# Interleaved attention and FFN block: the order of the work lists of TensorE, ScalarE and VectorE

## The reference

```python
xn = _layernorm(x)
# attention, on _rmsnorm(xn, norm_w)
q = x @ Wq; k, v = split(x @ Wkv)               # 16 heads of 64
q = _head_rmsnorm(q, q_gamma); k = _head_rmsnorm(k, k_gamma)
sim = jnp.tanh(q @ k.T / 50.0) * 50.0 * 64 ** -0.5
out = (softmax(sim) @ v) @ Wo
# FFN, m1 and m2 are products of token rows of the batch
h = gelu(x @ W1.T + scale * (x @ m1.T) + b1)
ffn = h @ W2.T + scale * (h @ m2.T) + b2
return x + out + ffn
```

## Time and profile before

| | |
|---|---|
| median of three executions | 1172.26 us |
| the profiled execution | 1171.93 us, span 1170.0 us |
| granted clock of TensorE | 0.996 of full speed |
| PE busy | 1053.4 us (90%) |
| ACT busy | 1033.3 us (88%) |
| DVE busy | 932.8 us (80%) |
| POOL busy | 853.8 us (73%) |

### The profile page before, as it was taken

One profiled execution on the slowest core, in us unless ns is written; L12 is line 12 of the kernel. 1 busy time (PEld: TensorE's weight loads), 2 busy tenths in 40 slices (PEclk: granted clock), 3 DMA queues, 4 the chain that ended last, 5 costly groups with the idle time before them and its releaser, 6 DMA issues.

```text
span 1170.0 us, 33883 instructions
## 1 busy us (share of the span) xinstructions
PE 1053.4 (90%) x12873; PEld 833.1 (71%) x12873; DVE 932.8 (80%) x2185; ACT 1033.3 (88%) x1543; POOL 853.8 (73%) x784
## 2 busy tenths in 40 slices
PE   3779999999999999999999999999999999999987
PEld 2457777777777777777777777777777777777766
DVE  5887878887878878878878878878888878888862
ACT  2689999999999999999999999999999999999886
POOL 6577777778778777778777778777778777778654
PEclk9899999999999999999999999999999999999999
DMA  4244443334433333434334433334333334343341
GB/s 142 42 78 67 77 74 77 68 74 74 77 77 74 70 70 78 74 75 77 72 66 79 76 72 79 66 74 79 74 72 78 71 69 83 70 75 70 71 81 33
DMA packets 310743, 86.45 MB, mean 74 GB/s; under 512 B 282036, under 2 KB 309816, under 8 KB 310584
## 3 DMA queue, kind: packets, MB, share of 16 engines
q1 hardware_dynamic: 310584, 84.30, 37.7%
HBM read 12.13 MB, written 4.19 MB: 14 GB/s over the span
## 4 chain that ended last, share of the span: by engine, by line
ACT 34%; PE 26%; DVE 26%; issue 12%; DMA 0%; POOL 0%; ACTq 0%
ACT clamped L569 12%; PE ps_scores L492 9%; DVE qk L764 7%; ACT probs L576 7%; PE ps_aux L467 5%; DVE halves L728 5%; ACT oT L608 4%; ACT L613 4%; DVE o_sb L741 3%; PE ps_y L542 3%; DVE v_lo L769 3%; DVE norm L679 3%; ACT hid L613 3%; PE ps_y L540 3%; PE ps_aux L426 2%
## 5 line engine op out<-in xcount | busy, mean ns | idle before, releaser
L931 POOL TENSOR_TENSOR probs_lo<-probs 128x1024 f16<-128x1024 f32 x256 | 484.7, 1893 | 270.3 <-ACT probs L576 270.3
L569 ACT ACTIVATE clamped<-ps_scores 128x1024 f32<-128x1024 f32 x256 | 265.9, 1039 | 67.2 <-PE ps_scores L492 66.9
L576 ACT ACTIVATE probs<-clamped 128x1024 f32<-128x1024 f32 x256 | 275.4, 1076 | 1.0 <-PE ps_o L522 0.4
L728 DVE TENSOR_TENSOR halves<-ps_n,halves 128x512 f16<-128x512 f32 x256 | 175.1, 684 | 99.3 <-ACT halves L584 99.2
L520 PEld LDWEIGHTS ps_o<-v_hi,probs 128*128 128x128 bf16 x2048 | 184.7, 98 | 90.0 <-issue 87.5
L520 PE MATMUL ps_o<-v_hi,probs 128*128 128x65 bf16 x2048 | 214.0, 195 | 33.2 <-DVE ps_n L720 23.1
L492 PE MATMUL ps_scores<-heads_T 64*128 64x256 f16 x3072 | 212.8, 271 | 6.9 <-ACT clamped L569 4.7
L521 PE MATMUL ps_o<-v_lo,probs 128*128 128x64 bf16 x2048 | 212.2, 193 | 0.0
L522 PE MATMUL ps_o<-v_hi,probs_lo 128*128 128x65 bf16 x2048 | 211.9, 194 | 0.0
L426 PE MATMUL ps_aux<-w_hi,xhT_hi 128*128 128x512 f32 x384 | 174.4, 454 | 40.0 <-DVE v_lo L769 25.6
L521 PEld LDWEIGHTS ps_o<-v_lo,probs 128*128 128x128 bf16 x2048 | 187.5, 99 | 0.0
(11 more groups left out here) (80 smaller groups left out, 1919.4 us busy)
## 6 DMA issues: line engine op xcount, KB each, us to landing
heads_T<-halves SPq DMA_TRANSPOSE x512, 2.5
x_in<-in_L_attn_tokens_dram SPq DMA_DIRECT2D x32, 128.0 KB, 2.3
x_res<-in_L_attn_tokens_dram SPq DMA_DIRECT2D x32, 128.0 KB, 2.3
out_dram<-y_sb SPq DMA_DIRECT2D x32, 128.0 KB, 2.0
sel_raw<-xn SPq DMA_DIRECT2D x192, 4.0 KB
qk<-in_L_attn_Wkv_dram SPq DMA_DIRECT2D x2, 512.0 KB, 5.2
qk<-in_L_attn_Wq_dram SPq DMA_DIRECT2D x1, 512.0 KB, 4.0
qk<-in_L_ffn_W_dram SPq DMA_DIRECT2D x2, 256.0 KB
```

The costliest lines, as they stand in the source:

```text
L569: nc.scalar.activation(clamped[:].rearrange("p j n -> p (j n)"), ps_scores[:].rearrange("p j n -> p (j n)"), ACT.Tanh).then_inc(clamp_done, 1)
L576: nc.scalar.activation(probs[:, pair % RING].rearrange("p j n -> p (j n)"), clamped[:].rearrange("p j n -> p (j n)"), ACT.Exp, bias=LIFT, ...
L728: v.tensor_tensor(halves16[:, pair % 4, 1].rearrange("p a n -> p (a n)"), ps_n[:], halves16[:, pair % 4, 0].rearrange("p a n -> p (a n)"), ...
L931: g.tensor_tensor(probs_lo[:, buf].rearrange("p j n -> p (j n)"), probs[:, buf].rearrange("p j n -> p (j n)"), probs[:, buf].rearrange("p ...
```

## The change

Three tables are written anew, and the code that walks them is adapted.

PE: `AUX` and `Y_PRODUCTS` become one table, `TENSOR_STEPS`, in which the output products (`"y"`, with their number) stand among the auxiliary tasks. In slots 1 and 2 two of the four products now stand ahead of the second oT task. In slot 6 two products stand between k 1 and v 2 (before: one, behind v 3), in slot 7 there are three instead of four. `AUX`, in which the order and the banks are the same as before, is derived from the table.

ACT: the high half for slot 4 is made in slot 3 between exp and the gelus; the cast of v 1 goes from slot 6 (between tanh and exp) to the end of slot 5.

DVE: the low half for slot 4 goes to the end of slot 3. In slot 0, q 3 goes ahead of the normalise. Sum 3 goes from slot 0 into slot 7 before it, sum 4 from slot 1 to 0, sum 6 from slot 2 to the end of slot 1, sum 1 from slot 5 to slot 6, sum 7 in slot 2 behind the normalise; both seeds stand ahead of low 1; in slot 6, v 1 goes ahead of the divide.

```diff
+TENSOR_STEPS = [
...
+    [("scores",), ("values",), ("xT", 0, 2), ("low", 0, 0), ("y", 2), ("oT", 1, -1), ("y", 2)],
...
-    [("half",), ("tanh",), ("oT", 3, -1), ("exp",), ("hid", 0, 0), ("hid", 1, 0)],
-    [("half",), ("tanh",), ("exp",), ("q", 0, 2)],
...
+    [("half", 3), ("tanh",), ("oT", 3, -1), ("exp",), ("half", 4), ("hid", 0, 0), ("hid", 1, 0)],
+    [("tanh",), ("exp",), ("q", 0, 2)],
...
-    [("halves",), ("q", 2, 1), ("divide",), ("normalise",), ("q", 3, 1), ("result",), ("sum", 3, 1)],
...
-    [("halves",), ("sum", 6, 1), ("sum", 7, 1), ("divide",), ("normalise",), ("seed", 0), ("low", 1, 0), ("seed", 1)],
...
-    [("halves",), ("divide",), ("normalise",), ("v", 3, 1), ("sum", 2, 2)],
+    [("halves", 3), ("q", 2, 1), ("divide",), ("q", 3, 1), ("normalise",), ("result",), ("sum", 4, 1)],
...
+    [("halves", 3), ("divide",), ("normalise",), ("sum", 7, 1), ("seed", 0), ("seed", 1), ("low", 1, 0)],
...
+    [("halves", 3), ("divide",), ("normalise",), ("v", 3, 1), ("sum", 2, 2), ("sum", 3, 2)],
...
-Y_PRODUCTS = {1: 4, 2: 4, 3: 3, 4: 4, 5: 4, 6: 1, 7: 4}
...
-                    for task in aux_tasks(st, s):
-                        aux(st, *task)
-                    if "back" in st.stages and s in Y_PRODUCTS:
-                        result(st, sum(Y_PRODUCTS.get(i, 0) for i in range(s)), Y_PRODUCTS[s])
+                    for what, *k in TENSOR_STEPS[s]:
...
+                        elif what == "y":
+                            if "back" in st.stages:
+                                result(st, made, k[0])
+                            made += k[0]
...
-                            normed = ahead_of(st, s, NORMALISE_LEAD - 1)
+                            normed = ahead_of(st, s, *k)
```

More of the change, by code:

```diff
@@ L50 @@
 AUX_BANKS = 3
-AUX = [
[3 rows of a table removed]
-    (3, "hid", 0, 0), (3, "hid", 1, 0),
[4 rows of a table removed]
+TENSOR_STEPS = [
[3 rows of a table added]
+    [("scores",), ("values",), ("hid", 0, 0), ("hid", 1, 0), ("y", 3)],
[4 rows of a table added]
 ]
+AUX = [(s, *task) for s, tasks in enumerate(TENSOR_STEPS) for task in tasks if len(task) == 3]
 assert len(AUX) % AUX_BANKS == 0
@@ L72 @@
 SCALAR_STEPS = [
-    [("half",), ("tanh",), ("q", 3, 1), ("exp",), ("k", 2, 1), ("k", 3, 1)],
-    [("half",), ("tanh",), ("oT", 0, -1), ("exp",), ("xT", 0, 2)],
-    [("half",), ("tanh",), ("oT", 1, -1), ("exp",), ("oT", 2, -1)],
-    [("half",), ("tanh",), ("oT", 3, -1), ("exp",), ("hid", 0, 0), ("hid", 1, 0)],
-    [("half",), ("tanh",), ("exp",), ("q", 0, 2)],
-    [("half",), ("tanh",), ("q", 1, 2), ("exp",), ("v", 0, 1)],
-    [("half",), ("tanh",), ("v", 1, 1), ("exp",), ("k", 0, 2), ("k", 1, 2), ("v", 2, 1)],
@@ L80 @@
-    [("half",), ("tanh",), ("v", 3, 1), ("exp",), ("q", 2, 2)],
+    [("half", 3), ("tanh",), ("q", 3, 1), ("exp",), ("k", 2, 1), ("k", 3, 1)],
+    [("half", 3), ("tanh",), ("oT", 0, -1), ("exp",), ("xT", 0, 2)],
+    [("half", 3), ("tanh",), ("oT", 1, -1), ("exp",), ("oT", 2, -1)],
+    [("half", 3), ("tanh",), ("oT", 3, -1), ("exp",), ("half", 4), ("hid", 0, 0), ("hid", 1, 0)],
+    [("tanh",), ("exp",), ("q", 0, 2)],
+    [("half", 3), ("tanh",), ("q", 1, 2), ("exp",), ("v", 0, 1), ("v", 1, 1)],
@@ L81 @@
+    [("half", 3), ("tanh",), ("exp",), ("k", 0, 2), ("k", 1, 2), ("v", 2, 1)],
+    [("half", 3), ("tanh",), ("v", 3, 1), ("exp",), ("q", 2, 2)],
 ]
 VECTOR_STEPS = [
-    [("halves",), ("q", 2, 1), ("divide",), ("normalise",), ("q", 3, 1), ("result",), ("sum", 3, 1)],
-    [("halves",), ("sum", 4, 1), ("divide",), ("normalise",), ("sum", 5, 1), ("xT", 0, 2), ("low", 0, 0)],
-    [("halves",), ("sum", 6, 1), ("sum", 7, 1), ("divide",), ("normalise",), ("seed", 0), ("low", 1, 0), ("seed", 1)],
-    [("halves",), ("divide",), ("newton", 0), ("normalise",), ("newton", 1), ("newton", 2), ("newton", 3), ("newton", 4)],
@@ L87 @@
-    [("halves",), ("divide",), ("newton", 5), ("newton", 6), ("newton", 7), ("newton", 8), ("normalise",), ("norm_stats",),
+    [("halves", 3), ("q", 2, 1), ("divide",), ("q", 3, 1), ("normalise",), ("result",), ("sum", 4, 1)],
+    [("halves", 3), ("divide",), ("normalise",), ("sum", 5, 1), ("sum", 6, 1), ("xT", 0, 2), ("low", 0, 0)],
+    [("halves", 3), ("divide",), ("normalise",), ("sum", 7, 1), ("seed", 0), ("seed", 1), ("low", 1, 0)],
+    [("halves", 3), ("divide",), ("newton", 0), ("normalise",), ("newton", 1), ("newton", 2), ("newton", 3), ("newton", 4),
+     ("halves", 4)],
@@ L88 @@
+    [("divide",), ("newton", 5), ("newton", 6), ("newton", 7), ("newton", 8), ("normalise",), ("norm_stats",),
      ("q", 0, 2)],
-    [("halves",), ("divide",), ("normalise",), ("q", 1, 2), ("sum", 0, 2), ("sum", 1, 2), ("v", 0, 1)],
-    [("halves",), ("divide",), ("v", 1, 1), ("normalise",), ("v", 2, 1)],
-    [("halves",), ("divide",), ("normalise",), ("v", 3, 1), ("sum", 2, 2)],
+    [("halves", 3), ("divide",), ("normalise",), ("q", 1, 2), ("sum", 0, 2), ("v", 0, 1)],
+    [("halves", 3), ("v", 1, 1), ("divide",), ("normalise",), ("sum", 1, 2), ("v", 2, 1)],
@@ L316, in wait_bank, with aux_index @@
                     return
[L318 to L321, removed]
+        def aux_index(kind, k):
+            return [(what, n) for _, what, n, _ in AUX].index((kind, k))
         def bank_of(kind, k):
-            i = [(what, n) for _, what, n, _ in AUX].index((kind, k))
+            i = aux_index(kind, k)
             return ps_aux[:, i % AUX_BANKS, :]
@@ L548, in run @@
                     pe.wait_ge(consts_loaded, 16 * 3)
+                made = 0
                 for s in range(PAIRS):
[L550 to L554, removed]
-                    for task in aux_tasks(st, s):
-                        aux(st, *task)
-                    if "back" in st.stages and s in Y_PRODUCTS:
-                        result(st, sum(Y_PRODUCTS.get(i, 0) for i in range(s)), Y_PRODUCTS[s])
+                    for what, *k in TENSOR_STEPS[s]:
+                        if what == "scores":
+                            if "attn" in st.stages:
+                                scores(st, s)
+                        elif what == "values":
+                            late = pair_of(st, s, VALUES_LAG)
+                            if late:
+                                values(st, s, *late)
+                        elif what == "y":
+                            if "back" in st.stages:
+                                result(st, made, k[0])
+                            made += k[0]
+                        elif STAGE[k[1]] in st.stages:
+                            aux(st, aux_index(what, k[0]), what, *k)
             run_all(pe, run)
```

## The result

The changed kernel takes 1117.62 us (median of four, 1116.06 to 1118.71); the ratio to the kernel before is 0.9545, 95% interval 0.9527 to 0.9563. 1112 was predicted. Its profiled execution took 1117.5 us with a span of 1115.5.

The account below looks back on a forecast made before the run. PE, with its stalls, was taken to set the pace outside slots 3 and 4, which belong to ACT. Gains 0.50+0.13+0.86+0.23+0.20 = 1.92 us a period, over 31 periods 59.5 us, gave 1112 us; range 1090 to 1146.

Parts of the forecast that it names:

- The wait before v 1: PE before v 1: it would now wait 1.0 us there for q 0's scaling, so only 0.13 us arrives.
- y between the oT transposes: PE, slots 1 and 2: two y products fill the 0.25 us idle before oT; 3.93 becomes 3.68 each, gain 0.50.
- The estimate by the figure of the Trainium skill: PE, slots 1, 2 and 6: an open 107 ns load at each added switch makes the period 0.32 us longer, total 1122.
- Slots 3 to 5: PE stalls of 0.36 and 0.76 us go, but ACT has no gap there; 13.08 becomes 12.95, gain 0.13.
- the clock: The prediction's time scale in us, starting at slot 3's tanh on ACT.
- the moved half only trades places with the gelus: ACT, slots 3 and 4: 0.46 in, 0.46 out, some hundredths more; q 0's square still starts at 9.02.
- Slot 6: PE's wait for v 1's low part, about 1.1 us, shrinks by the earlier v 1 and two y products; gain 0.86.
- No cost, with 0.4 to spare: ACT, slot 6: despite v 1's earlier cast, ACT is ready for slot 7's tanh at 17.5, PE's scores at 17.9.
- Slots 7 and 0: PE: three y products for four in slot 7, gain 0.23; q 3 scaled earlier on DVE for slot 0, gain 0.20.
- take over: Rival: DVE's full row from q 0 to q 3 delays k 3 and oT 0; period 33.6, 1130 us; chance 0.18.
- POOL was not late: Rival, slot 7: sum 3 waits for POOL's squares; if 3.2 us late, +1.2 a period, 1211 us; slower, chance 0.04.
- Freed PE time: Rival, slots 3 to 5: v 1 is freed as PE needs it, about 0.7 more; period 32.3, 1090 us; chance 0.12.

## Why the prediction was right

*What bounds the kernel.* Right for the change as a whole: what was taken out of slots 1, 2, 6, 7 and 0 came out in the period, and the stall removed before the values of slot 5 did not, because ACT was full there. The runs with the half moved alone and undone show it directly. As a rule ("each 0.1 us of stall removed there is 0.1 us of the period") it is too strong: the 0.64 us of slots 1 and 2 came back in slot 3 where the seed was late, and so did the 0.19 us of slot 0. The 2.6 us in six slots behind it were 2.1 in five. The wait before v 1 came where it was put (1.0 expected; 502.32+0.24 to 503.48 is 0.92, of which the row shows 0.76, since it counts from a modelled end).

*y between the oT transposes.* Right, and undersized: 0.64 instead of 0.50. Of the 0.07 us that each slot gave beyond 0.25, 0.05 is the transposes, which take 0.44 in the stream and took 0.49 behind the stall. The split costs nothing that shows, where 0 to 0.09 each was allowed. The estimate by the figure of the Trainium skill, "TensorE: Matmul & The Clock Gate", section "LDWEIGHTS (loading the stationary operand)", 1122 us, lies as near to the measured time as the forecast does, but not for its reason: 107 ns showed at neither switch of slot 1, where the groups start 0.44 apart as in the stream. But the prediction counted this gain as belonging to slots 1 and 2 alone. The run with the output products alone shows that the gain needs the earlier seed as well: without it slot 3 takes all 0.64 of it back. The prediction booked the sums and the seed at 0.36 us in slots 3 to 5, which then vanished behind ACT; undone, they cost 0.64 us a period, inside slots 1 and 2's term. The parts overlap elsewhere too: undone one at a time they cost 0.84 (output products), 0.50 (v 1), 0.59 (q 3), 0.64 (sums and seed) and -0.08 us (half), 2.5 us together, and the change gains 1.72. Only two parts were run alone.

*Slots 3 to 5.* 12.95 was expected, 13.12 measured, so the term came out as a loss of 0.04 us and not a gain of 0.13. v 1 starts at 10.45 on the clock instead of 10.36. 0.07 of that is ACT's square of q 0, at 9.09 instead of 9.02: "the moved half only trades places with the gelus" left out a wait. The half starts 1.03 us after exp, not 0.96, since it waits for the normalise of slot 3, which DVE ends at 495.42:

```profile
494.73 0.69 DVE L726 TENSOR_TENSOR ps_n<-qk,ps_o 128x512 f32<-128x512 f32 x1
```

The other 0.09 is PE's: after the stall v 1 and the products take 1.78 us to the scores, where 1.69 was counted (528.62 less 526.93, an unstalled start).

*Slot 6.* 5.01 expected, 5.17 measured. "No cost, with 0.4 to spare" looked at the last instruction of ACT's slot and not at k 0's copy in the middle of it, which v 3 waits for. ACT's tanh, exp and copies there:

```profile
506.82 1.09 ACT L575 ACTIVATE clamped<-ps_scores 128x1024 f32<-128x1024 f32 x1
507.94 1.06 ACT L582 ACTIVATE probs<-clamped 128x1024 f32<-128x1024 f32 x1
508.90 1.06 ACT L606 COPY qk<-ps_aux 128x512 f32<-128x512 f32 x2
```

The cast of v 1 stood ahead of this copy before, too, but between tanh and exp. Exp reads what tanh wrote and starts only at its end, 1.12 us after its start (506.82 to 507.94), where the prediction counted 0.92. With the cast between them exp starts 1.38 after tanh (the run with v 1 as before), so the cast cost 0.26 there and costs 0.47 at its new place. The copy starts 15.87 on the clock, against 15.65 in that run, and v 3 starts 0.38 after its predecessor instead of 0.23. v 1's low part did what was said: undone, it costs 0.50 us. The two output products ahead of v 2 were undone only together with all the others.

*Slots 7 and 0.* Right to the hundredth (3.73, 3.97), and undoing q 3's place cost the 0.60 expected. The hundredth of slot 0 is partly luck: k 3 is done at 24.2 and q 3's scaling at 24.45 on the clock, both some 0.4 later than the 23.75 and 24.1 of the prediction, and only their distance counts.

*The rivals.* DVE's row is tight but did not take over: sum 3 in slot 7 costs before oT 0 what it gains before the seed. It does set slot 0, as the run with q 3 put back shows. POOL was not late: its squares end at 513.43, 20.4 on the clock, and the sums that need them start at 513.88. Freed PE time did not arrive by itself, as the run with q 0 early shows.

The miss of 5.6 us is for the most part 0.20 us a period times 31, which is 6.2; the start and the last batches, for which nothing was counted, gained some 1.3 us. The 0.20 itself is what is left of errors in both directions: 0.14 too little in slots 1 and 2, 0.17 and 0.16 too much in slots 3 to 5 and in slot 6. That they partly cancel is luck.

## What to carry to other kernels

In a kernel whose engines each walk a written list, price a moved instruction at the next place where its consumer's list stands still, not at the stall it removes: the largest wait here (1.0 us before v 1) was worth nothing alone, and a wait of 0.36 us was worth 0.64 as soon as another part had made PE earlier. Test parts both alone and undone; where the two differ, as with the output products (0.50 alone, 0.84 undone), look for a second wait right behind. And when an operation is put ahead in a list, look at every consumer of what it pushes back, the ones in the middle too.

## What the runs showed of the hardware

A stall costs more than its idle time. The first f32r product after a stall starts 0.34 us ahead of the next (503.48 to 503.82), in an unstalled stream 0.23 to 0.24, behind fp32 output products 0.31 (508.61 to 508.92). Four transposes take 0.49 us after a stall (510.13 to 510.62) and 0.44 in the stream (520.76 to 521.20). An ACT operation that reads what the one before it wrote starts at that one's end: exp 1.12 us after the start of tanh (506.82 to 507.94), while an independent cast starts after 0.92 (510.52 to 511.44); so a cast or copy of 0.46 between the two delays exp by 0.26 only. And a releaser named by the trace can be a bystander: the wait put down to POOL's low part was the seed's, 0.08 us earlier.
